# A first transposed load in two halves, and thirteen constant products instead of ten ahead of the first real ones

## The reference

```python
scale = cond @ norm_w.T + 1.0
ms = jnp.mean(x * x, axis=-1, keepdims=True)
h = x * (scale[:, None, :] * jax.lax.rsqrt(ms + EPS))
u = h @ up_w.T
val, gate = jnp.split(u, 2, axis=-1)
h = val * jax.nn.gelu(gate, approximate=False)
hq = act_quant(h)            # per token to integers of 8 bits
wq = weight_quant(down_w)    # ternary, one scale for the whole weight
y = hq @ wq.T
return y + x
```

## Time and profile before

| | |
|---|---|
| median of 3 runs | 426.82 us (426.65 to 427.75) |
| the profiled execution, its own time | 427.15 us |
| its span, first to last instruction | 425.3 us |
| TensorE busy (PE) | 421.2 us, 99% of the span |
| VectorE, ScalarE, GpSimd busy | 66%, 44%, 39% |
| share of the chain that ended last | PE 98%, DMA 1% |

### The profile page before, as it was taken

One profiled execution on the slowest core, in us unless ns is written; L12 is line 12 of the kernel. 1 busy time (PEld: TensorE's weight loads), 2 busy tenths in 40 slices (PEclk: granted clock), 3 DMA queues, 4 the chain that ended last, 5 costly groups with the idle time before them and its releaser, 6 DMA issues.

```text
span 425.3 us, 7673 instructions
## 1 busy us (share of the span) xinstructions
PE 421.2 (99%) x2086; PEld 338.3 (80%) x2086; DVE 279.8 (66%) x538; ACT 187.7 (44%) x335; POOL 165.2 (39%) x323
## 2 busy tenths in 40 slices
PE   8999999999999999999999999999999999999997
PEld 6878888788888788887888887888878888878786
DVE  4886656756657656567566576565675665765676
ACT  6764344444444443444443444434444434444441
POOL 2644433433424424334334244343344343443320
PEclk9999999999999999999999999999999999999999
DMA  8434544433443324443334434243433344342324
GB/s 267 186 61 114 126 99 108 114 72 101 103 119 99 94 81 121 99 112 110 77 96 114 108 99 105 76 116 99 119 103 75 97 123 99 99 116 70 85 51 125
DMA packets 82088, 45.01 MB, mean 106 GB/s; under 512 B 68256, under 2 KB 68768, under 8 KB 81952
## 3 DMA queue, kind: packets, MB, share of 16 engines
q1 hardware_dynamic: 81792, 44.60, 40.4%
q10 hardware_dynamic: 288, 0.33, 0.3%
HBM read 20.00 MB, written 8.39 MB: 67 GB/s over the span
## 4 chain that ended last, share of the span: by engine, by line
PE 98%; DMA 1%; DVE 0%; issue 0%; DVEq 0%
PE p_gate L768 41%; PE p_val L768 41%; PE p_y L788 13%; DMA cond_norm_sb<-cond_norm 1%; PE p_gate L693 0%; PE p_y L678 0%; PE p_gate L699 0%; PE p_gate L705 0%; DVE y_sb L531 0%; PE p_val L746 0%; PE p_gate L746 0%; PE p_val L752 0%; PE p_gate L752 0%; PE p_val L705 0%; PE p_val L693 0%; PE p_val L699 0%
## 5 line engine op out<-in xcount | busy, mean ns | idle before, releaser
L625 DVE SCALAR_TENSOR_TENSOR h<-p_val,rstd,gelu 128x512 f32<-128x512 f32 x124 | 92.4, 745 | 127.6 <-PE p_val L768 126.7
L426 ACT ACTIVATE gelu<-p_gate,rstd 128x512 f32<-128x512 f32 x124 | 84.9, 684 | 141.9 <-PE p_gate L768 134.7
L299 POOL TENSOR_TENSOR mean_sq_eps<-mean_sq,rms_eps 128x1 f32<-128x1 f32 x64 | 12.2, 191 | 235.0 <-ACT squares L360 235.0
L372 ACT ACTIVATE q<-q_rounded 128x1024 bf16<-128x1024 f32 x63 | 66.6, 1058 | 79.2 <-DVE q_rounded L592 79.2
L768 PE MATMUL p_gate<-up_hi,a_lo 128*128 128x512 f32 x248 | 80.6, 406 | 0.0
L768 PE MATMUL p_val<-up_hi,a_hi 128*128 128x512 f32 x248 | 78.2, 396 | 0.0
L768 PE MATMUL p_val<-up_hi,a_lo 128*128 128x512 f32 x248 | 78.1, 396 | 0.0
L768 PE MATMUL p_val<-up_lo,a_hi 128*128 128x512 f32 x248 | 78.1, 396 | 0.0
L768 PE MATMUL p_gate<-up_lo,a_hi 128*128 128x512 f32 x248 | 78.1, 395 | 0.0
L768 PE MATMUL p_gate<-up_hi,a_hi 128*128 128x512 f32 x248 | 78.1, 395 | 0.0
L578 DVE TENSOR_REDUCE h_max<-h 128x1 f32<-128x1024 f32 x63 | 76.5, 1214 | 1.2
(11 more groups left out here) (87 smaller groups left out, 252.4 us busy)
## 6 DMA issues: line engine op xcount, KB each, us to landing
xt_in<-x_t SPq DMA_DIRECT2D x32, 256.0 KB, 2.8
x_all<-x SPq DMA_DIRECT2D x32, 256.0 KB, 2.9
out<-y_sb SPq DMA_DIRECT2D x31, 256.0 KB, 2.0
up_raw<-up_w_t SPq DMA_DIRECT2D x7, 256.0 KB, 5.4
down_raw<-down_w_t SPq DMA_DIRECT2D x1, 1024.0 KB, 7.9
q_t<-q SPq DMA_TRANSPOSE x63, 3.1
up_raw<-up_w_t ACTq DMA_DIRECT2D x1, 256.0 KB, 3.1
out<-y_sb SPq DMA_DIRECT2D x1, 128.0 KB, 2.0
```

What stands on the lines that cost most here:

```text
L299: pool.tensor_tensor(mean_sq_eps[:, j:j + 1], mean_sq[:, j:j + 1], rms_eps[:, :], ALU.add).then_inc(pool_step, 1)
L372: act.activation(q[j % 2][:, :], q_rounded[j % 2][:, :], ACT.Copy, bias=-ROUND).then_inc(q_ready, 1)
L426: act.activation(gelu[c][:, :], p_gate[c][:, :], ACT.Gelu, scale=rstd[:, j:j + 1]).then_inc(gelu_done, 1)
L625: nc.vector.scalar_tensor_tensor(h[s][:, c * W:(c + 1) * W], p_val[c][:, :], rstd[:, j:j + 1], gelu[c][:, :], op0=ALU.mult, op1=ALU.mult). ...
```

## The change

The first batch of `x_t` comes in two loads, one for each half k of the contraction, each of 128 rows of 1 KB instead of 2 KB. Each has a semaphore of its own, `first_xt_in[k]`. `a_hi` of tile 0 (VectorE) and of tile 1 (ScalarE) wait for half k before they work on it, rather than for the whole. The semaphore `xt_landed[0]` has no part in the first load any more, so GpSimd's loop waits for 16u of it instead of 16(u + 1). And TensorE runs thirteen constant products instead of ten before it waits for `cond_norm`.

```diff
+        first_xt_in = [sem(f"first_xt_in{k}") for k in range(KD)]
...
             sp.dma_start(cond_norm_sb[:, :], cond_norm).then_inc(cond_norm_in, 16)
-            load_xt(0, 0)
+            for k in range(KD):
+                sp.dma_start(xt_in[0][:, k, :, :].rearrange("p j q -> p (j q)"),
+                             x_t[0, :, k, :, :].rearrange("p j q -> p (j q)")).then_inc(first_xt_in[k], 16)
             load_up(0, 1)
...
-                    if j % TPB == 0:
+                    if j == 0:
+
+                        pool.wait_ge(xt_landed[0], 16 * u)
+                    elif j % TPB == 0:
...
-            act.wait_ge(xt_landed[0], 16)
             for k in range(KD):
+                act.wait_ge(first_xt_in[k], 16)
                 act.wait_ge(scale_ready, k + 1)
...
-            dve.wait_ge(xt_landed[0], 16)
             for k in range(KD):
+                dve.wait_ge(first_xt_in[k], 16)
...
-            keep_busy(10)
+            keep_busy(13)
```

## The result

The changed kernel takes 427.99 us, the median of 21 runs (427.71 to 428.99). The kernel before, run beside it again, takes 427.52 us (426.49 to 428.28, 21 runs). The ratio is 1.0016 with an interval of 1.0010 to 1.0022: the change makes the kernel slower by 0.16%, which is 0.5 us by the medians and 0.7 us by the ratio. The forecast was half a microsecond the other way. The measured time lies outside the stated range (425.8 to 427.3), but not all of that distance is the change's: the forecast started from 426.82, the median of three runs, and 21 runs of the same kernel have 427.52. Of the 1.69 us between the forecast (426.3) and 427.99, 0.70 are this starting point.

A forecast was written before the change was run, and what follows sets the result against it. PE was taken as bound by its own work from 3.48 us on. Profiled 427.15 - 0.58 (early clock rise, capped by `h`) + 0.05 (later landings) = 426.62, less 0.33 to the median: 426.3 us, range 425.8 to 427.3.

The forecast's parts named there:

- What bounds the kernel: Whole span: PE, busy 99%, bound by its own work from 3.48 us on; start changes carry to the end.
- The clock: PE at the start: filling the gap makes the clock rise at 5.7 us instead of 8.4.
- the filled pause: PE ahead of the scale's products: three more constant products fill 0.40 us idle, so work is unbroken from 0.78.
- The cap by `h`: Value part of `second_block`: waits for the first `h`, starts at 13.10 at the earliest, so the gain is 0.58 us.
- The split's cost: SP's queue at the start: loads issued up to 0.49 us later, mostly hidden by DMA backlog; 0 to 0.05 us.
- Rival B: SP's queue: extra slot delays weight landings; +0.29 us with the old clock, 0.09 gain left with early rise; chance 0.12.
- the four rivals: Alternatives at the start: clock rise unmoved (0.29), late weight landings (0.12), constant products overrun (0.08), load not waited for.
- Rival C: PE at the start: constant products overrun, scale and all real products 0.23 us later at the same clock, 427.05; chance 0.08.
- The term of 0.02: PE at the start: thirteen constant products delay the scale's products from 3.48 to 3.50; upper end 0.23 us.
- The split's gain: VectorE's `a_hi` of tile 0 starts up to 0.30 us earlier, but PE is held by fillers: worth 0.00 us.

The follow-up runs named there:

- fill_only: The kernel before with thirteen constant products instead of ten, first load whole; 426.50 us, ratio 0.9992.
- after_again: The changed kernel run once more, nothing altered; 427.93 us, ratio 1.0020 against the kernel before.
- split_same_count: The changed kernel with the last two up weight pieces in one load, so SyncE's queue holds as many instructions as before; 427.83 us, ratio 1.0018.
- h_first: fill_only with five constant products behind the scale instead of six, and the first `h` ahead of low part (3, 0); 426.72 us, ratio 0.9994.
- split_only: The changed kernel with ten constant products instead of thirteen, so the load in two halves alone; 428.06 us, ratio 1.0024.
- before_again: The kernel before once more, unchanged, one execution; 427.35 us.
- before_third: The kernel before a third time, unchanged, one execution; 427.83 us.
- small_load_first: tail_shift with its 4 KB load moved to right behind the first load of `x_t`; 427.85 us, ratio 1.0021.
- halves_by_rows: The changed kernel with the halves cut by partitions, 64 each in rows of 2 KB, both awaited before the first `a_hi`; 429.06 us, ratio 1.0046.
- tail_shift: fill_only with one more load, 4 KB that nobody reads, behind all other start loads on SyncE's queue; 427.09 us, ratio 1.0001.
- short_rows: fill_only with the first `x_t` in one load into an extra tile with a gap, giving rows of 1 KB; 427.62 us, ratio 1.0020.

## Why the prediction was wrong

**What bounds the kernel.** Right. A microsecond at the start is a microsecond at the end, up to the last product: the value part of `second_block` is 0.72 later and the last group of products 0.84. But "a change at the start is worth exactly what it moves the point from which PE never waits again" left out what comes behind the last product.

**The clock.** Right that it rises earlier with thirteen constant products; the time of the rise was luck. The changed kernel shows products 0.26 apart at 5.90, forecast 5.7, but the rise moves from execution to execution. The six constant products behind the scale show it: at the lower level they take 1.46 us, at the upper one 0.84. In fill_only, after_again and split_same_count (timeline, PE, of each):

```profile
4.21 1.46 PE L678 MATMUL p_y<-const-bfloat16-1.0 128*128 128x256 bf16 x6
4.21 0.95 PE L684 MATMUL p_y<-const-bfloat16-1.0 128*128 128x256 bf16 x6
3.91 0.84 PE L684 MATMUL p_y<-const-bfloat16-1.0 128*128 128x256 bf16 x6
```

Over the ten traces with thirteen constant products the upper pace begins between about 3.6 (split_same_count, h_first) and 6.6 (fill_only), in seven of them before 5.0; over the four with ten (before three times, split_only) between 7.8 and 9.5. The two groups don't overlap. What about the three products does it the runs don't show. The reason given in the prediction, the filled pause, was weaker than the result: in before_again and before_third the scale's products came at 3.01 and 3.00 with hardly a pause, and the rise was late all the same. The Trainium skill, TensorE: Matmul & The Clock Gate (What you observe), has the rise about 4 us into sustained work, give or take half a microsecond. Counted from the first product at 0.78 that is 4.8, inside the spread measured with thirteen, but the spread is about three times as wide as the page's, and with ten constant products no trace is near it; the measurement decides.

**The cap by `h`.** Right as a mechanism. PE waits for `h` in the changed kernel, 0.67 and 0.55 us in its two traces, at the place named, and the time of the rise made no difference behind it: value parts at 12.98, 13.00 and 13.21 belong to rises at 6.6, 5.3 and 4.2. The cap itself moved, from 13.10 to 14.40 and 13.87, and what moved it is the failed term, the next one.

**The split's cost, "I take 0 to 0.05 us with 0.49 as the far end".** This step failed. Its reason was that a later issue is hidden while the DMA engines are behind with their work, read from a share of 0.92 at 8 us and from the four microseconds between issue and use. What the runs show in its place: the three pieces behind the first load took 4.0, 4.2 and 5.0 us from issue to landing before and 4.3, 4.5 and 5.9 after, though they were issued later, so nothing of the delay was hidden. Over all traces with rows of 2 KB and no further issue in front (seven) piece (0, 1) is used at 5.48 to 6.00 and piece (1, 1) at 7.04 to 7.79; with one more issue in front (small_load_first, split_only, the changed kernel twice, split_same_count; halves_by_rows is left aside) at 6.06 to 6.50 and 7.93 to 8.97. In the means that is 0.6 and 0.8 us later for 0.47 us of issue. The four microseconds between issue and use were no sign of slack: even the 4 KB load took 3.3 us right behind the first one, and 7.6 us behind all others. How much of the 3.3 is backlog isn't shown. The share of the DMA engines couldn't have told it either: in the trace before it is 0.98 from 4.50 to 7.00, around these uses, higher than the 0.92 that the prediction took from 8 us.

**Rival B** named the mechanism: the slot of SP's queue reaches the landings, +0.29 with the late clock, or 0.09 of gain left with the early one, a value part at 13.59. For the issue alone that was well sized: small_load_first has it at 13.42. What B left out is that the two halves cost more than their slot (13.87 and 14.40), and the end. None of the four rivals had the whole.

**What no step had.** One more load on SyncE's queue makes the last store late, 0.33 in its issue and up to 0.3 in its landing. Its price in tail_shift is 0.6 us. The kernel that I forecast at 426.3 had this in it whatever the landings did.

**The sum by the runs.** fill_only 426.50; the end adds 0.6 (tail_shift 427.09); the issue in front adds 0.76 (small_load_first 427.85); the changed kernel is at 427.93 to 427.99. By these medians hardly anything is left for the halves themselves and their short rows. But they come from three chips, and the traces divide it otherwise: 0.42 at the value part for the issue in front, and 0.45 to 0.98 more with the two halves; short_rows alone cost about 1.0. So it is shown that the split costs 1.4 us (after_again against fill_only, one chip) and that it does so through late weight pieces and a late last store. How the first part divides between the extra issue and the rows of 1 KB is open.

Rival C, constant products that overrun: the scale's products came at 3.64 and not at 3.50, and in fill_only too. The term of 0.02 was 0.16, between its two ends. Next to before_again and before_third, whose scale came at 3.01 and 3.00, it is 0.6: the pause of 0.40 that the change was to fill belonged to that one execution. Behind the early clock it costs nothing that the times show.

**The split's gain** was forecast at 0.00, rightly: with the issue of the second half 0.47 later, `a_hi` of half k = 1 came at 5.56 and 5.29 in the two traces of the changed kernel instead of 4.94 on VectorE before, so there it even turned into a loss (in split_only it came at 4.70).

## What to carry to other kernels

Ahead of loads that someone waits for, an issue isn't free because the DMA engines look busy. Neither a long time from issue to landing nor a high share of the DMA engines shows that a later issue is hidden: here both stood in the trace before, and the loads came later all the same. Price an issue in front at its own time at least, unless a run shows that it is hidden. Cutting a load in two to get the first half sooner has to pay for what it does to the loads behind it; here they had no slack. After any edit that adds an instruction to a queue, look at the last microseconds of the trace too, even where the code there hasn't changed. And where a kernel's times scatter by more than the effect, three runs are too few to start a forecast from, and one trace too few to take a pause or a rise of the clock for a property of the kernel.

## What the runs showed of the hardware

The issue of the first load of `x_t`, 256 KB, took 0.42 us on SyncE's queue with 128 rows of 2 KB and 0.67 us with 256 rows of 1 KB; a load of 128 KB took 0.42 us with 128 rows of 1 KB, but two of 128 KB on 64 partitions each took 1.20 us together, so the count of rows alone doesn't give it. A load of 4 KB took 0.42 us to issue as well. Weight pieces that were issued 0.47 us later were used 0.6 to 0.8 us later in the mean over five traces against seven. The queue's last two stores stand 0.51 to 0.52 us apart in all eight traces of kernels with the old count of instructions on that queue, and 0.85 to 0.86 in the six with one more; what happens in the extra 0.33 us stays open. TensorE went from the pace of 1.2 GHz to that of 2.4 GHz between 3.6 and 6.6 us with thirteen constant products ahead and between 7.8 and 9.5 with ten. The windows printed a granted clock of 1.00 throughout, also where products of 512 columns stood 0.43 us apart, the pitch of 1.2 GHz.
